# Residual and shared-expert output added to the expert sums in DRAM instead of in SBUF

## The reference, cut to what matters

```
x = layernorm(x + attention(x))                # 3 heads, full width
x = layernorm(x + cross_attention(x, ctx))     # 16 heads, causal       -> called x2 below
logits  = x2 @ gate_w.T                        # 64 experts
scores  = softmax(logits); topk_w, topk_idx = top_k(scores, 6)
# each expert takes at most CAP = 128 of the (token, choice) pairs, in token order
d[e]    = (silu(buf[e] @ w_gate[e]) * (buf[e] @ w_up[e])) @ w_down[e]
y[t]    = sum over the 6 choices of topk_w * d[expert, slot]
y[t]   += (silu(x2 @ sh_gate.T) * (x2 @ sh_up.T)) @ sh_down.T      # shared expert
out     = layernorm(x2 + y)
```

## Time and profile before

| | |
|---|---|
| median of three runs | 2343.31 us |
| profiled execution, its own time | 2345.75 us |
| span of its trace | 2344.0 us |
| PE (TensorE matmul) busy | 2062.7 us, 88% |
| DVE (VectorE) busy | 1759.2 us, 75% |
| ACT (ScalarE) busy | 980.6 us, 42% |
| POOL (GpSimd) busy | 772.8 us, 33% |
| DMA | 268.71 MB, mean 115 GB/s |

### The profile page before, as it was taken

One profiled execution on the slowest core, in us unless ns is written; L12 is line 12 of the kernel. 1 busy time (PEld: TensorE's weight loads), 2 busy tenths in 40 slices (PEclk: granted clock), 3 DMA queues, 4 the chain that ended last, 5 costly groups with the idle time before them and its releaser, 6 DMA issues. The chain is left out here.

```text
span 2344.0 us, 50221 instructions
## 1 busy us (share of the span) xinstructions
PE 2062.7 (88%) x17648; PEld 1307.3 (56%) x17648; DVE 1759.2 (75%) x3790; ACT 980.6 (42%) x1515; POOL 772.8 (33%) x631
## 2 busy tenths in 40 slices
PE   7989899899889989989998953699999999999960
PEld 3556565566556556655655632466666666666640
DVE  5458888888788888878888877467777677776758
ACT  4324443443344344334433423355455554555533
POOL 1002412431342243134124314344444444454420
PEclk9999999999999999999999975799999999999985
DMA  6821001001100100110010041578788887877846
GB/s 215 110 110 40 11 29 38 18 20 38 38 9 29 38 19 19 38 38 9 29 38 12 17 142 52 149 238 247 228 251 238 244 247 229 250 238 245 247 131 243
DMA packets 132885, 268.71 MB, mean 115 GB/s; under 512 B 32304, under 2 KB 42544, under 8 KB 132848
## 3 DMA queue, kind: packets, MB, share of 16 engines
q1 hardware_dynamic: 108176, 226.13, 30.2%
q0 software_dynamic: 20480, 33.71, 7.2%
q10 hardware_dynamic: 4192, 8.39, 0.9%
HBM read 217.12 MB, written 51.12 MB: 114 GB/s over the span
## 5 line engine op out<-in xcount | busy, mean ns | idle before, releaser
L677 POOL TENSOR_SCALAR_AFFINE_SELECT x_plus_shared<-x_plus_shared 128x1024 f32<-128x1024 f32 x64 | 82.6, 1291 | 840.3 <-ACT x_plus_shared L889 840.1
L702 PE MATMUL ring<-xT_split,tion_then_expert_weights 128*128 128x256 f16 x2304 | 269.0, 274 | 7.5 <-POOL xT_split L655 3.8
L702 PE MATMUL ring<-tion_then_expert_weights,xT_split 128*128 128x512 f16 x1152 | 273.4, 390 | 1.4 <-issue 1.3
L873 ACT ACTIVATE x_plus_shared<-ring 128x512 f16<-128x512 f32 x224 | 130.2, 595 | 341.9 <-PE ring L702 309.0
L107 POOL DMA_INDIRECT slot_table<-table_records,slot_of_choice x192 | 228.3, 1189 | 86.0 <-issue 54.9
L702 PEld LDWEIGHTS ring<-xT_split,tion_then_expert_weights 128*128 128x128 f16 x2304 | 221.5, 98 | 45.0 <-issue 16.3
L702 PEld LDWEIGHTS ring<-tion_then_expert_weights,xT_split 128*128 128x128 f16 x1152 | 112.7, 100 | 138.8 <-issue 18.9
L991 DVE CUSTOM_DVE_ANT_0 quad<-quad,causal_penalty 128x128 f32<-128x128 f32 (+1 forms) x512 | 164.7, 394 | 30.7 <-PE quad L772 28.5
L1232 POOL DMA_INDIRECT expert_sums<-tion_then_expert_weights,scatter_index x64 | 151.4, 2365 | 59.0 <-POOL scatter_index L1229 55.7
L1007 DVE RECIPROCAL inv_denominator<-ring 128x256 f32<-128x256 f32 x64 | 111.9, 1749 | 68.7 <-PE ring L702 58.1
L953 DVE SCALAR_TENSOR_TENSOR x_plus_shared<-ring,x_plus_shared 128x512 f16<-128x512 f32 x192 | 130.3, 685 | 26.9 <-ACT x_plus_shared L873 26.3
(11 more groups left out here) (198 smaller groups left out, 4195.8 us busy)
## 6 DMA issues: line engine op xcount, KB each, us to landing
tion_then_expert_weights<-in_w_gate SPq DMA_DIRECT2D x64, 704.0 KB
tion_then_expert_weights<-in_w_up SPq DMA_DIRECT2D x64, 704.0 KB
tion_then_expert_weights<-in_w_down SPq DMA_DIRECT2D x64, 512.0 KB, 3.9
tion_then_expert_weights<-in_w_down SPq DMA_DIRECT2D x64, 192.0 KB, 4.0
xT_in<-in_xT SPq DMA_DIRECT2D x16, 512.0 KB, 4.4
x_in<-in_x SPq DMA_DIRECT2D x16, 512.0 KB, 3.4
expert_sums<-zero_rows SPq DMA_DIRECT2D x16, 512.0 KB, 12.9
x_rows<-x_plus_shared SPq DMA_DIRECT2D x16, 512.0 KB, 2.8
```

The source lines that it names most:

```text
L677: pool.affine_select(out=p32[:, g % 2, :, 0:2 * P], in_=p32[:, g % 2, :, 0:2 * P], compare_op=ALU.is_ge, fill=0.0, base=0, pattern=[[0, 4] ...
L702: last = pe.matmul(out_, left(a, c), right(b, c), start=(n == 0), stop=(n == 3 * chunks - 1))
L873: act.activation(half(0), src, ACT.Copy, scale=scale).then_inc(high, 1)
```

## The change

Three edits. The expert sums in DRAM are no longer filled with zeros: SyncE stores each sequence's x2 twice, to `x2_d` and to `moe_d`. In `experts` the load of x2 rows is gone; VectorE evicts SD with its scale alone into a new tensor of 128 rows, `sd32`, and GpSimd adds that to the rows i*128 on of `moe_d` by a direct accumulating transfer, between the two indirect ones: it waits for SD's eviction and for slot 0's accumulation, and slot 1's accumulation waits for it. VectorE's eviction of SD waits for the previous body's transfer. In `finish` the addition of `z` is gone. `z` was also staging space earlier; that space stays, as `scratch`.

```diff
@@ attend, SyncE
-                for r in range(0, T, 2 * P):
-                    sp.dma_start(moe_d[r:r + 2 * P, :].rearrange("(p r) n -> p (r n)", r=2), w["zeros"][:, :])\
-                      .then_inc(filled, 16)
-                    n += 1
...
-                    sp.dma_start(x2_d[bass.ds((i - 2) * N, N), :].rearrange("(t p) e -> p t e", p=P),
-                                 x2[:, :, :]).then_inc(x2_stored, 16)
+                    for d in (x2_d, moe_d):
+                        sp.dma_start(d[bass.ds((i - 2) * N, N), :].rearrange("(t p) e -> p t e", p=P),
+                                     x2[:, :, :]).then_inc(x2_stored, 16)
...
-            sp.wait_ge(x2_stored, 16 * B + 1)
+            sp.wait_ge(x2_stored, 32 * B + 1)
@@ attend, VectorE
-                            dve.wait_ge(x2_stored, b.n(0, 0, 16, 17 if b.c else 1))
+                            dve.wait_ge(x2_stored, b.n(0, 0, 32, 33 if b.c else 1))
@@ experts, SyncE
-                if not first:
-                    sp.wait_ge(free, freed(i - 1, "SD", 0))
-                sp.dma_start(x2n[:, :], x2_d[bass.ds(i * P, P), :]).then_inc(x2n_in, 16)
@@ experts, GpSimd, add
                 for s in range(2):
+                    if s == 1:
+                        pool.wait_ge(free, freed(i, "SD", 0))
+                        pool.wait_ge(added, 48 * i + 16)
+                        own_wait(pool, taken)
+                        pool.dma_start(moe_d[bass.ds(i * P, P), :], sd32[:, :], accum_op=ALU.add).then_inc(added, 16)
                     pool.wait_ge(free, freed(i, "D", s))
 
                     if not (first and s == 0):
-                        pool.wait_ge(added, 32 * i + 16 * s)
+                        pool.wait_ge(added, 48 * i + 32 * s)
...
-            pool.wait_ge(added, 32 * BODIES)
+            pool.wait_ge(added, 48 * BODIES)
@@ experts, VectorE
-                            dve.wait_ge(added, 32 * i + (16 * s - 16))
+                            dve.wait_ge(added, 48 * i + (32 * s - 32))
...
-                        dve.wait_ge(x2n_in, 16 * i + 16)
-                        dve.scalar_tensor_tensor(z[:, bass.ds(i, 1), :].rearrange("p o n -> p (o n)"),
-                                                 bank_of(step)[:, :], 1.0 / W_SCALE, x2n[:, :],
-                                                 ALU.mult, ALU.add).then_inc(free, 1)
+                        if not first:
+                            dve.wait_ge(added, 48 * i - 16)
+                        dve.tensor_scalar(sd32[:, :], bank_of(step)[:, :], 1.0 / W_SCALE, None, ALU.mult)\
+                           .then_inc(free, 1)
@@ finish, VectorE
-                dve.tensor_tensor(a[:, tile], a[:, tile], z[:, tile], ALU.add).then_inc(summed, 1)
-                dve.wait_ge(summed, n + 1)
```

More of the change, by code:

```diff
@@ L139, in build @@
         ident = m.sb("ident", [P, P], F32)
-        z = m.sb("x2_plus_shared", [P, T // P, E], F32)
-        z_cols = z[:, :, :].rearrange("p t n -> p (t n)")
+        z_cols = m.sb("scratch", [P, T // P * E], F32)[:, :]
         stage, col = {}, T // P * E
@@ L188, in build @@
         with ExitStack() as s:
-            experts(nc, Memory(nc, s), ident, z, loads, table, x2_d, x2T_d, table_d, moe_d, sdT)
+            experts(nc, Memory(nc, s), ident, loads, table, x2_d, x2T_d, table_d, moe_d, sdT)
         with ExitStack() as s:
-            finish(nc, Memory(nc, s), moe_d, z, out)
+            finish(nc, Memory(nc, s), moe_d, out)
 def prepare(nc, mem, ident, w, z_cols, xT, wq, wk, wv, fcT, fcb, xwqT, wkvT, woutT, gateT):
@@ L1098, with experts @@
              for s in ([(u[0].replace("U", "G"), u[1]), u] if u in MOE_UPS else [u])]
-def experts(nc, mem, ident, z, loads, table, x2_d, x2T_d, table_d, moe_d, sdT):
+def experts(nc, mem, ident, loads, table, x2_d, x2T_d, table_d, moe_d, sdT):
     BODIES = T // P
@@ L1117, in experts @@
     x2t = mem.sb("x2T_block", [P, 2, EC, P], F16)
-    x2n = mem.sb("x2_block", [P, E], F32)
+    sd32 = mem.sb("shared_out", [P, E], F32)
     silu32 = mem.sb("silu_out", [P, 2, F], F32)
@@ L1133, in experts @@
     w_low = mem.sem("expert_weight_low")
-    x2t_in, x2n_in = mem.sem("x2T_in"), mem.sem("x2_in")
+    x2t_in = mem.sem("x2T_in")
     index_ready = mem.sem("index_ready")
@@ L1416, in emit, with finish @@
                         dve.wait_ge(full, job(i, *step))
-                        dve.wait_ge(x2n_in, 16 * i + 16)
-                        dve.scalar_tensor_tensor(z[:, bass.ds(i, 1), :].rearrange("p o n -> p (o n)"),
-                                                 bank_of(step)[:, :], 1.0 / W_SCALE, x2n[:, :],
-                                                 ALU.mult, ALU.add).then_inc(free, 1)
+                        if not first:
+                            dve.wait_ge(added, 48 * i - 16)
+                        dve.tensor_scalar(sd32[:, :], bank_of(step)[:, :], 1.0 / W_SCALE, None, ALU.mult)\
+                           .then_inc(free, 1)
             bodies(dve, emit)
-def finish(nc, mem, moe_d, z, out):
+def finish(nc, mem, moe_d, out):
     TILES = [2, 4, 8, 8, 6, 4]
@@ L1437, in finish @@
     loaded = [mem.sem(f"rows_loaded{n}") for n in range(len(TILES))]
-    summed, scaled, normed = mem.sem("summed"), mem.sem("row_scales"), mem.sem("normed")
+    scaled, normed = mem.sem("row_scales"), mem.sem("normed")
     stored = mem.sem("rows_stored")
```

## The result

On one chip, nine executions each, the changed kernel took 2330.48 us (median; 2324.32 to 2339.88) and the kernel before 2339.98 us (2335.34 to 2346.21): ratio 0.9958, 95% interval 0.9941 to 0.9976, or 9.5 us less. Forecast were 17.4 us less. The new kernel's profiled execution took 2330.48 us of its own, span 2328.9; against the profiled execution before (2345.75) that is 15.3 us less. The two differences don't agree, since the execution profiled before is slower than all but one of the kernel's nine, and the one after is the median. The medians decide how much; the profiles show where.

What follows compares the result with a forecast made beforehand. TensorE was taken to bound experts and VectorE the last block. Finish -17.6, start -4.9 and tail +5.1, other terms 0, sum to -17.4 us: from the median 2343.31 to a forecast of 2326, range 2319 to 2336.

Steps and rivals of the forecast that it cites:

- the base of the sum: Whole kernel: median of the runs shown, 2343.31 us; less 17.4 it gives 2325.9, forecast as 2326.
- Finish, -17.6: Last block: six additions leave VectorE's unbroken chain, loads staying ahead; -17.6 us, or -12 if stores and loads collide.
- Start, -4.9: Second attend body: without fills TensorE's 3.75 us wait goes and 24 products take 2.78, not 4.45; -4.9 us (0 to -5.4).
- the ring of banks: Start of attend: banks that VectorE frees after the norm of x1; half a microsecond of the 5.4 us left to them.
- x2 stored twice, 0: Attend: 16 more transfers of 512 KB on SyncE's queue, nothing waiting closely behind them; 0 us.
- Tail, +5.1: Last experts body: slot 1's accumulation begins only when the new transfer has landed, with nothing covering it; +5.1 us.
- The estimate of 2.6 us: Tail: skill page's cost for a 256 KB transfer, 2.0 us plus bytes at 436 GB/s; sum would be 2.5 us lower.
- Experts, 0 for 31 bodies: GpSimd's queue: new transfer takes over waits on VectorE, lag none to 0.9 us; 0 us, ends 0 and +141.
- The bound, 5.7 us: Experts: latest landing assumed for an accumulation, 3.5 to 5.7 us after its issue.
- The 1.8 us in hand at D's eviction: Experts: slot 1's eviction of D due at 1754.2, slot 1's landing at 1752.4 at the latest.
- the slower rival: Experts: GpSimd's chain of three accumulations and two gathers becomes the bound, excess 2.4 us a body; about 2396 us, chance 0.12.
- The rule weighed in the forecast: Experts: VectorE's two-operand instruction blocks only GpSimd operations reading SBUF; the direct issue would last under 1.6 us, sum unchanged.

Runs made afterwards that it cites:

- run 3: Kernel before without VectorE's six additions in finish, x2 plus shared output left out of the result: 2301.47 us against 2318.95, ratio 0.9928.
- Run 9: Kernel before with its 16 zero fills issued twice, the second set into a DRAM tensor nothing reads: 2338.77 us against 2318.61, ratio 1.0082.
- run 1: Changed kernel with the 16 zero fills back at their old place, into a DRAM tensor nothing reads: 2309.41 us against 2318.95, ratio 0.9964.
- run 2: Kernel before with the 16 fills spread, one beside each store of x2 instead of all at the start: 2319.66 us against 2318.95, ratio 1.0003.
- run 12: Kernel before, unchanged, run once more for a profile on such a chip: 2318.86 us.
- run 4: Changed kernel with the last body's shared output kept in SBUF and added by VectorE in finish: 2301.93 us against 2318.95, ratio 0.9924.
- run 5: Changed kernel again, unchanged, beside its variants: 2308.76 us against 2320.55 for the kernel before, ratio 0.9958.
- run 11: Changed kernel with GpSimd copying the two index columns ahead of its waits, nothing else: 2304.48 us, ratio 0.9933 to the kernel before.
- run 6: Changed kernel with two buffers for slot 1's D, used in turn, loops unrolled by two: 2308.67 us, ratio 0.9942 to the kernel before.
- run 7: Changed kernel with two buffers for slot 1's D and the last body's shared output kept in SBUF: 2304.35 us, ratio 0.9929 to the kernel before.
- run 8: Changed kernel with a second direct accumulating transfer of 256 KB, adding zeros, behind the first: 2513.97 us, ratio 1.0833 to the kernel before.
- Run 10: Changed kernel with early index copies by GpSimd and the last body's shared output kept in SBUF: 2302.40 us against 2318.61, ratio 0.9924.

## Why the forecast was right in part

The time, 2330.5, lies in the range, but the gain of the medians is 9.5 us for 17.4. That the time came as near as 4.5 us is partly luck: the base of the sum, 2343.31, was a median of three executions and is 3.3 us above that of nine. By the steps:

- **Finish, -17.6: right.** -18.0 in the profile, -17.5 alone (run 3). Loads stayed ahead and stores did not collide.
- **Start, -4.9: the mechanism right, its price not what I took for granted.** The transpose came 4.73 us earlier, though `xT_in` is issued only 17 us earlier (100.20) and not 30, behind a fill of 128 rows that holds SyncE's queue for 16.85 us. The half microsecond that I took off for the ring of banks was lost at the first body's start instead, so that 4.9 came so near is luck. Run 9 shows that such a stall is kept in full. But (a) on the first chip 3.1 us were given back later in attend, and (b) the stall is at an edge: with 26 to 27 us of issue for the fills instead of 31.2 it isn't there (runs 1, 2, 12), so on those chips the term is zero. In the sum I used one execution's stall as a property of the kernel. The 3.1 us lie in TensorE's waits ahead of L802 and for L1008; why they grew is not settled. On the later chips the bodies' sum is 1196.9 to 1197.3 us in most profiles and 1200.2 in two (runs 4 and 5); with the profile after, that makes three of the nine of the changed kernel's kind and none of the five others. Whether x2's second store has a part in it wasn't told apart.
- **x2 stored twice, 0: right but for those three profiles.** 1196.9 us of bodies with both stores (run 11), 1197.3 with one (run 12).
- **Tail, +5.1: right in kind, 4.6 measured** (and 3.5 once the index copies leave the series, run 11 against run 12: 30.8 less 27.3). The estimate of 2.6 us by the Trainium skill ("DMA: Bandwidth & Descriptors", the cost of one transfer) is too low for this kind: from its issue to the next copy there are 4.3 us with no weight load beside it.
- **Experts, 0 for 31 bodies: this is the step whose working failed.** "The lag is so between none and 0.9 us, within the 1.5 that cost nothing" left out a wait and bounded a landing by a mean. The wait is the one of slot 0's copy for slot 1's landing (line 1227 before). By the forecast's own times that landing comes at up to 1752.4, 3.2 us behind the 1749.22 at which the copy was due; in the profile after, the copy is over 3 us behind in 14 bodies, at most 4.79 against 0.34. The bound, 5.7 us behind the end of the issue, is the mean of waits of which the longest is 6.3; slot 1's landing takes 3.0 to 7.2 us in run 5, 5.8 in the median. The 1.8 us in hand at D's eviction are so 0.8 to 0.9 at least in runs 1 and 5. That 31 bodies still cost 0 in the profiled execution after is in part luck: slot 1's eviction stands 5.3 us behind slot 0's, and the lag ends just below that.
- **And the 0 does not hold for every execution.** Run 4's profile has the landing catch up with the eviction, 5.6 us in all; seven of 16 executions lie 8 to 15 us above the fastest ones; with the index copies out of the series none of ten does, nor with two buffers any of eleven (runs 6 and 7). Run 8 shows from the other side that no room is left. So the slower rival named the place, and the price was small because the excess is 0.27 us a body where it comes, instead of 2.4. That it also made the seven long executions of the changed kernel itself is argued from this and not shown by a profile of one; in run 4's, 3 us of the excess are attend's.

Put together for the later chips: -17.5 + 0 + 4.6 = -12.9 where nothing stalls, up to some 10 us more time in the long executions. The fastest executions of runs 1 and 5 are 13.2 and 12.6 us below the fastest of the kernel before, the medians 9.5 and 11.8 below its medians. Run 11 gives -14.1: -17.5 and a tail of +3.5 make -14.0.

On the first chip the profiles give -18.0 (finish) - 1.6 (start less what attend gave back) + 4.6 (tail) = -15.0, against 15.1 between the spans; experts has no part in it. The medians differ by 5.8 us less, because the execution profiled before was 2345.75 - 2339.98 = 5.8 us above its median. No execution of it at the median has a profile, so which block made these 5.8 us is open. Of the 7.9 us between 17.4 and 9.5 only the 3.1 that attend gave back are located.

VectorE's two-operand splits and GpSimd: the new direct issue takes 0.93 to 0.965 us in all 32 bodies, also at 1733.23, inside VectorE's split of a gate weight from 1732.66 to 1734.29, whereas the indirect issue is still stretched from 1.58 to 3.04 us. The rule weighed in the forecast (the Trainium skill, "SBUF — State Buffer", shared port pair) agrees for the direct issue, with the room it promised: 0.95 us rather than the 1.6 to 3.5 I allowed. It was taken up by landings longer than my bound.

**A version that beats both.** Run 10, -16.2 us (ratio 0.9924), and run 11 with a simpler edit, -14.1, against -9.5 to -11.8 for the change as made. Run 4 has run 10's median but one execution of five at 2311.6. The last block in SBUF takes most of the tail back; with the early copies no long execution was seen in ten. Intervals of 10 and 11 overlap, so their order isn't shown. Run 10's (0.9910 to 0.9937) lies below those of runs 1 and 5 (from 0.9943 on), run 11's (to 0.9947) just touches run 5's, and both ratios are from another chip.

## What to carry to other kernels

- Moving work from a vector engine's unbroken chain to accumulating transfers gains all of the chain's share at once; what it costs is room in the queue that issues them, so add up that queue's whole series (copies, issues, landings) and compare it with the body. Follow it over the body's end, to the first step that waits for the last landing, and take the longest landing on the rows and not the mean. When the series comes to within a microsecond, forecast a spread of executions and not zero or the full stall, and look for what else can leave the series.
- A stall read from one execution belongs in the sum only with its margin: how much earlier would the load have to be for it to be gone, and does that vary. Here 5 us of issue time between chips made 3.75 us of stall come and go.
- The last body is where serial accumulations show in full; peel it and keep its last term on chip.

## What the runs showed that was not expected

- The same kernel takes 2340 us on one chip and 2319 to 2321 on three others; 21 us of it are in attend. On the first chip TensorE waits up to 2.5 us ahead of the products at L806 eight times with no releaser shown ("issue", 20.0 us in all); in run 12 that wait doesn't appear, and all waits ahead of L806 together are 8.8 us there against 37.8. The cause was not found.
- An accumulating transfer of 256 KB has a long tail of landing times, and the indirect one's is the longer. The two profiles of the result hold no landing times. In run 5 (the changed kernel), for L1221 (direct) and L1230 (indirect):

```profile
L1221 POOL DMA_DIRECT2D expert_sums<-shared_out x32: 931/952/967, 1487.8 to 2243.5; - x32
...
DMA to landing us min/median/max: 4.1/5.7/7.3
```

```profile
L1230 POOL DMA_INDIRECT expert_sums<-tion_then_expert_weights,scatter_index x64: 1580/1634/3193, 1482.0 to 2248.9; - x64
...
DMA to landing us min/median/max: 4.6/5.8/10.4
```

The first line of each has the issue's own duration in ns (least, median, most) and the times of the first and the last; the landing counts from the issue's start. In the kernel before (run 12) the indirect ones take 4.9, 7.4 and 9.0 us. So long landings did not come with the change: they were there before, but the landing of slot 1 had 9.7 us or more in hand until its next eviction, and now it has about one.
